# Attention inside a six-stage macaron block: softmax maxima split before the transpose, one more fold of the row sums, a shorter lead

## The reference, cut to what matters

```python
HEADS, HEAD_DIM = 16, 32          # x: (2, 2048, 512)
q = (x @ q_w.T).reshape(b, s, HEADS, HEAD_DIM).transpose(0, 2, 1, 3)
k = x @ k_w.T                     # one key head for all 16 query heads
v = x @ v_w.T
scores = jnp.einsum('bhqd,bkd->bhqk', q, k) * SCALE
attn = jax.nn.softmax(scores.astype(jnp.float32), axis=-1).astype(q.dtype)
out = jnp.einsum('bhqk,bkd->bhqd', attn, v)
return out.transpose(0, 2, 1, 3).reshape(b, s, HIDDEN) @ o_w.T
```

## Time and profile before

| | before |
|---|---|
| Time, median of 3 | 4881.05 us (4880.63 to 4883.40) |
| Time of the profiled execution | 4881.05 us |
| Span of its trace | 4879.5 us |
| PE busy | 4676.6 us, 96% of the span |
| DVE, ACT, POOL busy | 60%, 46%, 48% |
| Granted TensorE clock, mean | 0.974 |

### The profile page before, as it was taken

How to read it: one execution, slowest core, us unless ns; L and a number is a source line. 1 busy time by engine, 2 the same in 40 slices (tenths; PEclk the granted TensorE clock), 3 DMA queues, 4 the chain that set the end, 5 groups by cost and what they waited for, 6 DMA issues and landing times. The chain is left out here.

```text
span 4879.5 us, 89290 instructions
## 1 busy us (share of the span) xinstructions
PE 4676.6 (96%) x30668; PEld 3646.1 (75%) x30669; DVE 2928.3 (60%) x5643; ACT 2241.4 (46%) x4559; POOL 2327.1 (48%) x1772
## 2 busy tenths in 40 slices
PE   6999996999999999999998799999999999999999
PEld 4788885666666666666656588887899987689998
DVE  6222225789999999999965522222655558674444
ACT  4222224466666666666662322222544435453433
POOL 1545434178888888888870335451411016420000
PEclk8999997899999999999999899999999999999999
DMA  7223226657777777777766523332532221251110
GB/s 220 79 92 101 91 83 223 245 109 147 147 147 147 147 147 147 147 147 147 147 125 192 181 84 99 94 99 65 193 99 92 88 90 59 69 192 51 53 53 32
DMA packets 253579, 593.91 MB, mean 122 GB/s; under 512 B 31680, under 2 KB 85952, under 8 KB 228800
## 3 DMA queue, kind: packets, MB, share of 16 engines
q0 software_dynamic: 62224, 317.75, 28.9%
q1 hardware_dynamic: 191024, 271.73, 16.9%
HBM read 262.74 MB, written 121.63 MB: 79 GB/s over the span
## 5 line engine op out<-in xcount | busy, mean ns | idle before, releaser
L1452 POOL TENSOR_TENSOR attend_pairs<-attend_pt 128x1024 f32<-128x1024 f32 x512 | 1257.6, 2474 | 196.3 <-ACT attend_pt L1417 196.1
L1465 DVE TENSOR_REDUCE attend_mx<-attend_am_ps 128x1 f32<-128x512 f32 x2048 | 1251.6, 680 | 123.8 <-PE attend_am_ps L1325 120.5
L1417 ACT ACTIVATE attend_pt<-attend_sc_ps 128x512 f32<-128x512 f32 x2048 | 1039.7, 620 | 283.4 <-PE attend_sc_ps L1313 283.3
L1325 PE MATMUL attend_am_ps<-attention_kst,attend_qst 96*128 96x512 f32 x2048 | 859.2, 425 | 8.9 <-DMA attend_qst<-q_parts 8.7
L1313 PE MATMUL attend_sc_ps<-attend_qst,attention_kst 98*128 98x512 f32 x2048 | 816.3, 400 | 1.5 <-ACT attend_pt L1417 1.3
L1325 PEld LDWEIGHTS attend_am_ps<-attention_kst,attend_qst 96*128 96x128 f32 x2048 | 393.4, 192 | 239.2 <-DVE attend_mx L1465 123.3
L718 DVE TENSOR_TENSOR expert_ac<-expert_gu_ps,expert_gl 128x512 f32<-128x512 f32 x144 | 99.6, 692 | 670.7 <-ACT expert_gl L682 670.6
L1339 PE MATMUL attend_pv_ps<-attend_pt,attention_v 128*32 128x256 f32 x8192 | 493.6, 381 | 0.0
L1313 PEld LDWEIGHTS attend_sc_ps<-attend_qst,attention_kst 98*128 98x128 f32 x2048 | 389.8, 191 | 87.3 <-ACT attend_pt L1417 11.7
L1339 PEld LDWEIGHTS attend_pv_ps<-attend_pt,attention_v 128*32 128x32 f32 x8192 | 246.2, 110 | 211.5 <-ACT attend_pt L1417 46.2
L1820 ACT ACTIVATE ffn_sg<-ffn_gu_ps,ffn_gs 128x256 f32<-128x256 f32 x352 | 166.7, 474 | 508.2 <-PE ffn_gu_ps L1741 508.2
(11 more groups left out here) (347 smaller groups left out, 9126.4 us busy)
## 6 DMA issues: line engine op xcount, KB each, us to landing
attend_pairs<-attend_pairs POOLq DMA_DIRECT2D x189, 1024.0 KB, 7.4
weights_raw<-experts_dram POOLq DMA_DIRECT2D x76, 512.0 KB, 4.2
ys<-expert_ob SPq DMA_DIRECT2D x144, 256.0 KB, 2.3
attend_qst<-q_parts SPq DMA_DIRECT2D x192, 128.0 KB, 3.9
yn<-route_yb SPq DMA_DIRECT2D x64, 256.0 KB, 3.7
ffn_xb<-x SPq DMA_DIRECT2D x64, 256.0 KB, 2.8
ffn_rb<-x SPq DMA_DIRECT2D x64, 256.0 KB, 3.0
keyvalue_xb<-x SPq DMA_DIRECT2D x64, 256.0 KB, 2.8
```

The source lines that it names most:

```text
L1325: pe.matmul(am[:, bank, :], qst[0:KROWS, n % 2, h * HALF + hd, :], kst[0:KROWS, o:o + 4 * P], start=True, stop=True).then_inc(am_rdy, 1)
L1417: act.activation(pt[:, u % RING, g * 4 * P:(g + 1) * 4 * P], sc[:, s % SBANKS, :], ACT.Exp, scale=HD ** -0.5).then_inc(p_rdy, 1)
L1452: pool.tensor_tensor(pairs[:, slot(half, j), :], pt[:, 2 * p % RING, :], pt[:, (2 * p + 1) % RING, :], ALU.add).then_inc(pair_rdy, 1)
L1465: dve.tensor_reduce(mx[:, hh, block:block + 1], am[:, am_slot["max", a] % MBANKS, :], AX.X, ALU.max).then_inc(mx_rdy, 1)
```

## The change

It does five things in `attention_stage`:

1. A fourth fold after pair 13 (pair 5 of the next half) adds pair 1 onto pair 0, 512 KB. `sums` then reads pair 0 alone: 4 matmuls in place of 8. The last half isn't folded, before or now.
2. The high and low part of the maxima are made before the transpose: DVE reduces twice (once into `neg` at full precision, once into the rounded `msplit[:, 0]`) and subtracts (`msplit[:, 1]`, 128 x 8). PE transposes all 16 columns at once, and `keep` is one copy of 16 x 128.
3. LEAD goes from 28 to 24 units, and with it `split` (formerly `lowest`) moves from the end of batch A to the end of B, and the transpose with `keep` and the two DMAs from B to C.
4. The reciprocals are spread evenly: a piece after B, C, D and A, the output after A.
5. The second reduction waits for the transpose of the half before, which an extra count on `mT_rdy` at the start lets through for the first half.

```diff
-LEAD = 28
+LEAD = 24
-FOLD_AFTER = (4, 7, 10)
+FOLD_AFTER = (4, 7, 10, 13)
-SHARES_AT = ((0,), (1, 2), (3,), ())
...
-        mT = mem.sb("mT", [HALF, 2, P], F32R)
+        msplit = mem.sb("msplit", [P, 2, HALF], F32R)
+        mT = mem.sb("mT", [2 * HALF, P])
...
-            half, at = divmod(c + 3, PER_HALF)
+            half, at = divmod(c + 2, PER_HALF)
             return half if at == 0 and i == 3 and 0 <= half < HALVES else None
...
                     sp.dma_start(qst[row:row + 1, n % 2, h * HALF:(h + 1) * HALF, :].bitcast(F32),
-                                 mT[:, part, :].bitcast(F32)).then_inc(m_in[h], 16)
+                                 mT[part * HALF:(part + 1) * HALF, :]).then_inc(m_in[h], 16)
...
-                pe.wait_ge(neg_rdy, half + 1)
+                pe.wait_ge(ms_rdy, half + 1)
                 bank = am_bank(("turn", half))
-                pe.transpose(am[0:HALF, bank, 0:P], neg[:], const["ident"][:]).then_inc(mT_rdy, 1)
+                pe.transpose(am[0:2 * HALF, bank, 0:P], msplit[:].rearrange("p s h -> p (s h)").bitcast(F32),
+                             const["ident"][:]).then_inc(mT_rdy, 1)
...
                 pe.wait_ge(fold_in[-1], 16 * (half + 1))
-                for j in range(2):
-                    add_up(half, j, False, j == 1)
+                add_up(half, 0, False, True)
...
-                pool.wait_ge(pair_rdy, RING // 2 + half * HPAIRS + 2 * k + 4)
-                get = slot(half, 2 * k + 2)
-                pool.dma_start(pairs[:, to:to + 2, :], pairs[:, get:get + 2, :], accum_op=ALU.add).then_inc(fold_in[k], 16)
+                if k < len(FOLD_AFTER) - 1:
+                    pool.wait_ge(pair_rdy, RING // 2 + half * HPAIRS + 2 * k + 4)
+                    put, get = pairs[:, to:to + 2, :], pairs[:, slot(half, 2 * k + 2):slot(half, 2 * k + 2) + 2, :]
+                else:
+                    put, get = pairs[:, to, :], pairs[:, to + 1, :]
+                pool.dma_start(put, get, accum_op=ALU.add).then_inc(fold_in[k], 16)
...
-            def lowest(half):
+            def split(half):
                 h = half % 2
                 dve.wait_ge(mx_rdy, HPIECES * (half + 1))
-                dve.wait_ge(mT_rdy, half)
                 dve.tensor_reduce(neg[:], mx[:, h * HALF:(h + 1) * HALF, :], AX.X, ALU.max, negate=True).then_inc(neg_rdy, 1)
+                dve.wait_ge(mT_rdy, half + 1)
+                dve.tensor_reduce(msplit[:, 0, :], mx[:, h * HALF:(h + 1) * HALF, :], AX.X, ALU.max, negate=True).then_inc(neg_rdy, 1)
+                dve.wait_ge(neg_rdy, 2 * half + 2)
+                dve.tensor_tensor(msplit[:, 1, :], neg[:], msplit[:, 0, :].bitcast(F32), ALU.subtract).then_inc(ms_rdy, 1)
...
-                dve.tensor_copy(mT[:, 0, :], turned).then_inc(hi_kept, 1)
-                dve.wait_ge(hi_kept, half + 1)
-                dve.tensor_tensor(mT[:, 1, :], turned, mT[:, 0, :].bitcast(F32), ALU.subtract).then_inc(mT_kept, 1)
+                dve.tensor_copy(mT[:], am[0:2 * HALF, am_slot["turn", half] % MBANKS, 0:P]).then_inc(mT_kept, 1)
...
-                half, at = divmod(c + PER_HALF, PER_HALF)
+                half, at = divmod(c + 3, PER_HALF)
                 if at == 0 and 0 <= half < HALVES:
-                    lowest(half)
+                    split(half)
...
-                    for piece in SHARES_AT[at]:
-                        shares(half, piece)
-                    if at == 2:
+                    shares(half, at)
+                    if at == PIECES - 1:
                         output(half)
```

More of the change, by code:

```diff
@@ L1229, in attention_stage @@
         w_in, whi_rdy = mem.sem("w_in"), mem.sem("whi_rdy")
-        am_rdy, mx_rdy, neg_rdy, mT_rdy, hi_kept, mT_kept, s_rdy, p_rdy, pv_rdy, pair_rdy, sum_rdy, inv_rdy, o_rdy, vals_kept, sums_kept = (
-            mem.sem(n) for n in ("am_rdy", "mx_rdy", "neg_rdy", "mT_rdy", "hi_kept", "mT_kept", "s_rdy",
+        am_rdy, mx_rdy, neg_rdy, ms_rdy, mT_rdy, mT_kept, s_rdy, p_rdy, pv_rdy, pair_rdy, sum_rdy, inv_rdy, o_rdy, vals_kept, sums_kept = (
+            mem.sem(n) for n in ("am_rdy", "mx_rdy", "neg_rdy", "ms_rdy", "mT_rdy", "mT_kept", "s_rdy",
                                  "p_rdy", "pv_rdy", "pair_rdy", "sum_rdy", "inv_rdy", "o_rdy",
@@ L1458, in _ @@
         def _(dve):
+            dve.sem_inc(mT_rdy, 1)
             def maxi(a):
@@ L1465, in maxi @@
                 dve.tensor_reduce(mx[:, hh, block:block + 1], am[:, am_slot["max", a] % MBANKS, :], AX.X, ALU.max).then_inc(mx_rdy, 1)
-            def lowest(half):
+            def split(half):
                 h = half % 2
                 dve.wait_ge(mx_rdy, HPIECES * (half + 1))
-                dve.wait_ge(mT_rdy, half)
                 dve.tensor_reduce(neg[:], mx[:, h * HALF:(h + 1) * HALF, :], AX.X, ALU.max, negate=True).then_inc(neg_rdy, 1)
+                dve.wait_ge(mT_rdy, half + 1)
+                dve.tensor_reduce(msplit[:, 0, :], mx[:, h * HALF:(h + 1) * HALF, :], AX.X, ALU.max, negate=True).then_inc(neg_rdy, 1)
+                dve.wait_ge(neg_rdy, 2 * half + 2)
+                dve.tensor_tensor(msplit[:, 1, :], neg[:], msplit[:, 0, :].bitcast(F32), ALU.subtract).then_inc(ms_rdy, 1)
             def keep(half):
                 n, h = divmod(half, 2)
-                turned = am[0:HALF, am_slot["turn", half] % MBANKS, 0:P]
-                dve.wait_ge(mT_rdy, half + 1)
+                dve.wait_ge(mT_rdy, half + 2)
                 if half:
                     dve.wait_ge(m_in[1 - h], n * 32 + (32 if h else 0))
-                dve.tensor_copy(mT[:, 0, :], turned).then_inc(hi_kept, 1)
-                dve.wait_ge(hi_kept, half + 1)
-                dve.tensor_tensor(mT[:, 1, :], turned, mT[:, 0, :].bitcast(F32), ALU.subtract).then_inc(mT_kept, 1)
+                dve.tensor_copy(mT[:], am[0:2 * HALF, am_slot["turn", half] % MBANKS, 0:P]).then_inc(mT_kept, 1)
             def shares(half, piece):
@@ L1505, in _ @@
                         keep(turn_due(c, i))
-                half, at = divmod(c + PER_HALF, PER_HALF)
+                half, at = divmod(c + 3, PER_HALF)
                 if at == 0 and 0 <= half < HALVES:
-                    lowest(half)
+                    split(half)
                 half, at = divmod(c - 2 * PER_HALF - 1, PER_HALF)
                 if half >= 0:
-                    for piece in SHARES_AT[at]:
-                        shares(half, piece)
-                    if at == 2:
+                    shares(half, at)
+                    if at == PIECES - 1:
                         output(half)
-            for half in range(HALVES - 2, HALVES):
-                for piece in range(PIECES):
+            for half in range((BATCHES - 2 * PER_HALF - 1) // PER_HALF, HALVES):
+                for piece in range(max(0, BATCHES - PER_HALF * (half + 2) - 1), PIECES):
                     shares(half, piece)
```

## The result

The changed kernel takes 5025.64 us (median of 4 runs, 5021.12 to 5030.92) against 4880.84 us before: a ratio of 1.0297 with a 95% interval of 1.0279 to 1.0314, so 3% slower. Forecast were 4861.5 us and a range of 4845 to 4886. The profiled execution took 5021.55 us, with a span of 5019.9.

What follows compares the result with a forecast made beforehand. PE was taken to bound the kernel, busy for all 24.37 us of a half. 4881.05 - 28.0 (row sums) - 4.8 + 0.4 + 0.5 (ends) + 12.4 (waits for maxima) = 4861.5 us, range 4845 to 4886.

Steps and rivals of the forecast that it cites:

- Row sums, -0.445 us a half: PE in batch A: 8 records of row sums instead of 16, 0.445 us less in 63 halves, 28.0 us.
- POOL: 0.9 us a half: POOL between pairs 5 and 6: the extra DMA issue costs 0.9 us a half, nobody waits, taken as 0.
- The landing of the fourth fold: Batch A: the fold lands 0.6 to 2.5 us before PE's sums need it; taken as 0.
- The slower rival that rested on it: Batch A: sums wait for the fourth fold, up to 1 us a half, 63 us, giving 4925 us; chance 0.10.
- the whole list: DVE behind B: wait, two reductions, subtraction, reciprocal, 1.17 us at most, 0.93 with overlaps, against 0.92 of room; taken as 0.
- The batch with the transpose stays at 6.10: The transposing batch, B becoming C, keeps its 6.10 us despite the shorter `keep`: 0, at best -0.1 a half.
- The distance to the score: From the maxima's DMAs in C to the score in D: 5.55 us instead of 11.04; wait 0.2 us, +12.4 us.
- The tie with the fold: DMA queues at C + 5.2: maxima first, nobody waits; fold first, 0 to 0.2 us in most halves, 0.5 to 1.1 in some.
- The ends, -4.8 + 0.4 + 0.5: Stage start: eight fewer maxima, -4.8 us; stage end: maxima in one more batch, +0.4, and last fold's landing, +0.5.
- 4849 with no wait: Score in D: the maxima land in time everywhere, saving the 12.4 us, so 4849 us; chance 0.25.
- the wait in front of the score eats the gain: Score in D: B's fold ends next to C's, maxima go late, mean wait 0.4 to 0.7 us, 4883 us; chance 0.19.
- The whole-packet rule: DMA queues: the small DMA waits for the whole fold, the score about 2 us a half, 4973 us; chance 0.02.

Runs made afterwards that it cites:

- the fold alone: The kernel before with only the fourth fold added, 4 matmuls of row sums instead of 8, lead and maxima as before; 4900.53 us, ratio 1.0029.
- the kernel without the subtraction: The changed kernel with its 128x8 subtraction on DVE replaced by a third reduction of the same maxima; 4861.74 us, ratio 0.9950.
- the lead alone: The kernel before with LEAD 24, reduction behind B, transpose and both old copies in C, three folds; 4906.94 us, ratio 1.0047.
- one DMA: The changed kernel, subtraction kept, but only the high row of the maxima sent, in a single 4 KB DMA a half; 4951.34 us, ratio 1.0134.
- the change without the split: The changed kernel without part 2: LEAD 24, four folds, even spread, but old reduction, transpose of 8 and two copies; 4879.52 us, ratio 0.9989.

## Why the prediction was wrong

- **PE sets the pace, DVE has under 2 us to spare.** Right, and it is why 1.2 us on DVE could cost that much.
- **Row sums, -0.445 us a half.** Right: 0.46 us for 8 records (1764.94 to 1765.40), 568 records in place of 1072, and 24.36 against 23.92 us between three and four folds.
- **POOL: 0.9 us a half, taken as 0 since no consumer waits for the lag.** The size was right (in the fold alone an addition behind a fold ends 3.25 us after the one before it, two in a row 2.33), the 0 was not. The consumer is not one by a semaphore: DVE's two-input instructions are. In the fold alone this cost 0.6 us in every A. In the full change part 4 had moved the output away from there.
- **The landing of the fourth fold, taken as 0.** Nearly right: in the change PE's sums wait for it once, 2.9 us in the tail, and in the kernel without the subtraction nine times, 4.4 us in all. The slower rival that rested on it fell.
- **DVE: "For the subtraction the nearest rows are 0.19 (the reduction, the same 128x8 output) and 0.28", and of the whole list "I take 0, with 0.2 us a half as the upper end."** This is the step that failed. I priced it by work and bounded it with a row whose input was a bank of PSUM. That row is no neighbour: the right one was the output, the only DVE instruction in the stage with two SBUF inputs, and its row in the trace of before, 425 ns at the least and 1476 at the most for one and the same shape, said that something not shown held it. Measured: 1.40 us, 0.17 of it work. With 1.40 in the place of 0.19 the list of 0.93 to 1.17 us becomes 2.1 to 2.4, against a room of 0.92.
- **The batch with the transpose stays at 6.10.** Right without the subtraction (6.10), 7.22 with it.
- **The distance to the score.** Right as geometry: I had 5.55 us, it is 5.53 without the subtraction. The tie with the fold goes to the maxima when they leave 0.62 us ahead (no wait); at 0.3 us the score waits 0.25 to 0.4 us, as worked for the case that the fold is first. With the subtraction the DMAs leave 0.56 us after the fold: a third case, outside my two, in which both go late.
- **The ends, -4.8 + 0.4 + 0.5.** From the stage's start to its first score it was 33.4 us and is 28.6: right. From the start of half 62 to the last row sum it was 52.8 us and is 54.3, and 53.9 to 56.9 in the other kernels with a fourth fold: 1.1 to 4.2 us more where I had 0.9. Other kernels with three folds took 53.3 to 56.0, so this isn't the fold's alone, and its cause stays open.
- **The sum.** Without the failed step it was 4861.5, or 4849 with no wait; the kernel without the subtraction took 4861.74, while its ratio gives 4881 x 0.9950 = 4856.6. With it, 1.23 us became 2.49 us a half (26.41 - 23.92): 1.12 in C, where PE waits for banks, and 1.35 in D, where the DMAs had lost their place. The mean period is 2.67 longer, and 63 x 2.67 = 168 us, which is the 169 us between the two kernels. Most of what the mean has over the median stands in four halves, whose D takes 9.2 to 12.1 us, 14 us together over the 7.17 of the others (the last section says what happened there). (What lies outside the stage was 3284.5 to 3295.1 us in the profiled executions, with the same code, so single profiles are compared by the stage, and kernels by their medians.)
- **Rivals.** That the wait in front of the score eats the gain was the nearest, with 0.19, but by a fold that ends late; its real cause was upstream. I had no rival for an instruction that lasts longer than its work. The whole-packet rule would have shown in the kernel without the subtraction or in that of the lead alone; neither shows it.

## What to carry to other kernels

An instruction that is priced by its work must also be asked where its operands lie: here every DVE instruction with two SBUF inputs that began inside a GpSimd addition lasted past the end of that addition, and the profile books that as busy time and not as a wait. (Both were of the kind tensor_tensor. The one tensor_tensor that wasn't held had an input in PSUM, and 8 partitions; one with a PSUM input on 128 partitions wasn't tried.) A wide span between the shortest and the longest duration of one shape is the sign. And where a small DMA feeds the pacing engine, look at its place against the next large one as well as at its distance: here PE did not wait when the small DMA left 0.62 us ahead of the large one, and waited when it left 0.29 us ahead or 0.56 behind.

## What the runs showed that I had not expected

- A 128x8 subtraction on DVE took 0.17 us or 1.40 us, by what GpSimd did; the 8x128 subtraction with a PSUM input kept its 0.28 us in all runs (277 to 281 ns), and GpSimd was adding through the whole of it in 311 of 320 cases.
- What is left to do at the end of the addition is less than the whole instruction: the subtraction ends 0.035 us behind it and takes 0.166 alone, the output 0.285 behind it and takes 0.425 alone. So in both about 0.13 to 0.14 us run before the hold ends.
- GpSimd's additions are recorded as longer where the fourth fold is there and DVE is not late (means of 2.58 to 2.73 us in the seven kernels with four folds and a D of less than 6.1 us, 2.47 with three folds, 2.46 in the change itself and with one DMA). This is not more work. Pairs 6 and 7 are recorded with 3.01 and 2.99 us in the fold alone and with 2.39 and 2.38 before, yet the second starts 2.35 us behind the first in both: the records of two in a row overlap, by 0.65 us in the one and by 0.04 in the other. What sets the overlap wasn't tried.
- In the profiled execution of the change the granted clock fell to 1.2 GHz four times in the stage, for 3 to 7 us each (20 us together, near 1139, 1272, 1409 and 1545 us), and not once between 1000 and 2400 us in that of before. Each time PE stood idle for 1.6 to 3.3 us just before, or still did, where a score waited for the maxima; in the other halves that wait was about 1.1 us, and one of 1.6 had no fall beside it. Two more such falls, in the lead alone and in the change without the split, stand beside waits of 2.4 and 2.1 us. Longer waits and lower clock together are the 14 us of the four long batches D; the lower clock can account for about 10 of the 145 us. Why the maxima were later in these halves wasn't looked into.
